# A transformer layer on one core: weight units kept in order, low-rank rows moved by DMA, a new instruction order and no filler matmuls

## What is computed

```python
x = x + xattn(layernorm(x), ctx, ctx)     # 16 batches, 128 tokens, 512 features
x = x + ffn(layernorm(x))
# xattn: RMS norm of q (512) and k (128), rotary, 16 heads of 32 over 4 kv heads,
#        causal softmax, @ w_out.T
# ffn:   w = (w_q - 7.5) * repeat(scale, 64)          4-bit integers held as int32
#        h = relu(xn @ w_up.T + b_up + xn @ a_up @ b_up_lora)      2048 hidden units
#        y = h @ w_down.T + b_down + h @ a_down @ b_down_lora      rank 16
```

## Time and profile before

| | before |
|---|---|
| median of 3 runs | 496.49 us (496.36 to 497.72) |
| the profiled execution, its own time | 496.01 us |
| its span, first to last instruction | 494.2 us |
| PE busy in the span | 462.1 us, 94% |
| DVE, ACT, POOL busy | 348.2, 307.1, 281.3 us |
| mean granted TensorE clock | 0.969 |

### The profile page before, as it was taken

The page is one execution under the profiler, slowest core; times in us unless marked ns, Lnnn a source line. Parts: engine busy times, 40 slices in busy tenths (PEclk is TensorE's granted clock), DMA queues, the critical chain, the costliest instruction groups (busy, mean ns, idle before and its releaser), DMA issues.

```text
span 494.2 us, 8572 instructions
## 1 busy us (share of the span) xinstructions
PE 462.1 (94%) x2569; PEld 229.1 (46%) x2569; DVE 348.2 (70%) x1082; ACT 307.1 (62%) x928; POOL 281.3 (57%) x302
## 2 busy tenths in 40 slices
PE   0774899999999999999999999999999999999997
PEld 0752555545454444444444454545444444444443
DVE  2789999998868685868585868585858675633341
ACT  1499999776766666666676767666666756441110
POOL 3534757847685766565657575857575746460101
PEclk9977589999999999999999999999999999999999
DMA  6883589667786969595969696968787868374523
GB/s 149 313 236 63 183 195 257 104 116 149 140 141 122 173 127 166 99 174 98 197 97 196 98 185 109 175 119 172 115 169 118 158 115 135 76 145 82 86 50 98
DMA packets 207853, 70.43 MB, mean 143 GB/s; under 512 B 197808, under 2 KB 200112, under 8 KB 207120
## 3 DMA queue, kind: packets, MB, share of 16 engines
q1 hardware_dynamic: 205472, 69.33, 69.9%
q10 hardware_dynamic: 2256, 0.40, 0.5%
q0 software_dynamic: 80, 0.16, 0.1%
HBM read 17.44 MB, written 4.19 MB: 44 GB/s over the span
## 4 chain that ended last, share of the span: by engine, by line
PE 78%; DVE 3%; issue 0%
PE ff L949 33%; PE ff L933 32%; PE tb L913 7%; PE sb L881 2%; PE tb L899 2%; DVE big L1073 1%; PE ff L777 1%; DVE wd_lo L1081 1%; PE tb L865 0%; PE ff L837 0%; DVE pr L1179 0%; DVE y L1229 0%; DVE q L1188 0%; DVE z L1110 0%; DVE t_sin L1147 0%
## 5 line engine op out<-in xcount | busy, mean ns | idle before, releaser
L933 PE MATMUL ff<-wu_hi,xnT 128*128 128x512 f16 x512 | 152.4, 379 | 0.0
L949 PE MATMUL ff<-wd_hi,x 128*128 128x512 f16 x512 | 152.3, 379 | 0.0
L1179 DVE CUSTOM_DVE_ANT_0 pr<-sb,tabs,score_scale 128x128 f32<-128x128 f32 x256 | 73.8, 345 | 51.9 <-PE sb L881 51.9
L504 POOL TENSOR_TENSOR big<-pr,big 128x512 f16<-128x512 f32 x64 | 80.1, 1260 | 46.6 <-ACT big L704 46.3
L495 POOL TENSOR_TENSOR pr<-pr,rinv 128x512 f32<-128x512 f32 x64 | 72.0, 1126 | 60.4 <-DVE rinv L1089 60.3
L673 ACT ACTIVATE pr<-pr,nmax 128x128 f32<-128x128 f32 x256 | 98.9, 388 | 7.9 <-DVE nmax L1179 7.9
L933 PE MATMUL ff<-wu_lo,xnT 128*128 128x512 f16 x256 | 97.0, 379 | 0.0
L949 PE MATMUL ff<-wd_lo,x 128*128 128x512 f16 x256 | 97.0, 379 | 0.0
L738 ACT ACTIVATE hid<-z 128x512 f16<-128x512 f32 x64 | 40.0, 626 | 80.0 <-DVE z L1110 80.0
L933 PEld LDWEIGHTS ff<-wu_hi,xnT 128*128 128x128 f16 x512 | 48.2, 98 | 58.8 <-issue 5.9
L949 PEld LDWEIGHTS ff<-wd_hi,x 128*128 128x128 f16 x512 | 49.0, 98 | 54.3 <-DMA x<-hid 0.4
(11 more groups left out here) (153 smaller groups left out, 645.3 us busy)
## 6 DMA issues: line engine op xcount, KB each, us to landing
xt<-in_x SPq DMA_DIRECT2D x16, 256.0 KB, 3.1
big<-in_L_ffn_w_up_q SPq DMA_DIRECT2D x4, 1024.0 KB, 5.9
big<-in_L_ffn_w_down_q SPq DMA_DIRECT2D x4, 1024.0 KB, 5.6
out<-y SPq DMA_DIRECT2D x16, 256.0 KB, 3.0
kvt<-in_ctx SPq DMA_DIRECT2D x16, 64.0 KB, 2.6
wd_lo<-in_L_xattn_w_out SPq DMA_DIRECT2D x1, 1024.0 KB, 9.4
pT<-in_L_ffn_b_up SPq DMA_DIRECT2D x1, 1024.0 KB, 8.6
pT<-big SPq DMA_TRANSPOSE x64, 3.3
```

Of the source, the lines that this page charges most:

```text
L504: pool.tensor_tensor(p3[:, m, :, 1, :], pr[:, m], p3[:, m, :, 0, :], ALU.subtract).then_inc(p_low, 1)
L933: last = pe.matmul(bank[:], a[:, m, :], b[:, m, 512 * g:512 * g + 512], start=(m == 0 and i == 0), stop=(m == KC - 1 and i == 2))
L949: last = pe.matmul(ff[down_bank[n]][:], x2T[:, part, k + h % HG, :], b[:, h, :], start=(h == 0 and i == 0), stop=(h == HC - 1 and i == 2))
L1179: last = dve.tensor_tensor_reduce(pr[:, m, g, :], sbk[m % 2][:, P * g:P * g + P], mask, score_scale[:], 3e38, ALU.add, ALU.min, nmax[:, p, ...
```

## The change

The slot numbers are all new, with two fewer dequantisations and two fewer low parts on VectorE (`DVE_TILES` 26 to 24, `LOW_BY_DVE` 27 to 25). Besides:

```diff
-DVE_TILES = (0, 1, 2, 3, 4, 5, 6, 7, 8, 10, 11, 12, 13, 14, 15, 17, 18, 19, 21, 23, 25, 26, 27, 28, 29, 31)
+DVE_TILES = (0, 1, 2, 3, 4, 5, 6, 7, 9, 10, 11, 12, 13, 14, 15, 16, 17, 18, 21, 23, 25, 26, 27, 29)
+TURN_AT = (10, 30, 64, 91, 234, 258, 301, 449, 504, 516, 568, 619, 656, 687, 732, 750, 775, 784, 902, 976, 1017, 1035, 1078,
+           1084, 1111, 1165, 1188, 1341, 1653, 1726, 1791, 1792)
...
# SyncE: fewer loads first, another order, the rows by DMA
-            load_batch(0)
-            for src, dst in ((kw, kw_bc), (qw, qw_bc)):
+            sp.dma_start(s_dn[:], wds.rearrange("(c p) b -> p c b", p=P)).then_inc(scales_in, 16)
+            for src, dst in ((qw, qw_bc), (kw, kw_bc)):
...
-            for i in range(3):
-                sp.dma_start(b_up_in[R * i:R * i + R], wub).then_inc(b_in, 16)
-                sp.dma_start(b_dn_in[R * i:R * i + R], wdb).then_inc(b_in, 16)
-            sp.wait_ge(scales_in, 16 * 5)
+            load_batch(0)
+            sp.wait_ge(lora_a_in, 16 * 3)
+            sp.wait_ge(norm_w_in, 16 * 2)
             load_group(0)
+            sp.dma_start(wo_raw, wo.rearrange("(j p) c -> p j c", p=P)).then_inc(wout_in, 16)
             load_group(1)
             load_batch(1)
...
+                    if LORA_B_ROWS_AT[i] == s:
+                        sp.wait_ge(b_high, 2)
+                        sp.wait_ge(b_low, 2)
+                        for j in range(3):
+                            sp.dma_start(rows[R * j:R * j + R],
+                                         parts[:, j, :]).then_inc(moved, 16)
...
# ScalarE: low-rank splits on the flat form, 128 partitions; bias row contiguous
-                act.activation(dst, src, ACT.Identity, scale=kap[0:R3, kx:kx + 1]).then_inc(b_high, 1)
+                for parts, flat, kx in ((b_up_parts, b_up_flat, 4), (b_dn_parts, b_dn_flat, 5)):
+                    act.activation(parts[:, 0:2, :], flat.unsqueeze(1).broadcast_to([P, 2, flat.shape[1]]),
+                                   ACT.Identity, scale=kap[:, kx:kx + 1]).then_inc(b_high, 1)
...
# TensorE: no fill() anywhere, and in weights(t)
-                    rows = slice(P * j, P * j + P) if t < UP_TILES else slice(j, None, 4)
-                    last = turn(bank[:, P * i:P * i + P], stage[:, g % W_RING, i, rows],
+                    cols = slice(i, None, 4) if t < UP_TILES else slice(P * i, P * i + P)
+                    last = turn(bank[:, cols], stage[:, g % W_RING, i, P * j:P * j + P],
...
# VectorE: two low parts on the flat form, and another order of the scales
-            input_stats(0)
+            find_tops()
+            norm_powers()
+            gather_tops()
             norm_scales()
             input_moments(0)
-            find_tops()
-            spread_tops()
+            take_tops()
             find_scales()
```

More of the change, by code:

```diff
@@ L48 @@
[L48 to L58, removed]
@@ new lines @@
+R_MOMENTS = (0, 49, 395, 1329)
+R_KEYS = (0, 4, 268, 2190)
+R_POW = (2, 5, 1195, 2191)
+R_CENTRE = (3, 91, 546, 1587)
+R_SINES = (2, 84, 500, 1502)
+R_COSINES = (3, 45, 1206, 2313)
+R_ROPE = (4, 105, 687, 1553)
+R_KSPLIT = (4, 208, 900, 1660)
+R_KLOW = (5, 104, 827, 1624)
+R_KTURN = (259, 483, 1126, 1637)
+R_QSPLIT = (9, 256, 841, 1731)
+R_QLOW = (16, 115, 809, 1605)
+R_QTURN = (152, 503, 951, 1630)
+R_SCORES = ((88, 503, 1006, 1821), (99, 517, 1018, 1850), (124, 593, 1055, 1915), (243, 668, 1110, 1936))
@@ new lines @@
+R_PLOW = ((377, 1378, 2415, 2742), (417, 1440, 2498, 2838), (777, 1570, 2500, 2869), (890, 1619, 2505, 2876))
+R_PTURN = ((529, 1175, 1681, 2031), (741, 1232, 1708, 2041), (761, 1395, 1781, 2052), (798, 1397, 1783, 2058))
+R_VSUM = (496, 524, 922, 1902)
+R_VARG = (341, 433, 1200, 1802)
+R_VPOW = (632, 1469, 2457, 2773)
+R_VSPLIT = (670, 1269, 1936, 2193)
+R_VLOW = (971, 1827, 2712, 2951)
+R_PV = (745, 1312, 1980, 2264)
+R_OHIGH = (735, 1548, 2006, 2305)
+R_OLOW = (689, 1406, 1913, 2207)
+R_PROJ = (752, 1533, 1994, 2293)
@@ new lines @@
+LOAD_AT = (3, 282, 526, 863, 944, 1212)
+ROW_LOAD_AT, DOWN_BIAS_LOAD_AT = 7, 1179
+BATCH_LOAD_AT = (2, 777)
+LORA_BHIGH_AT, LORA_BLOW_AT = 5, 3
+LORA_B_ROWS_AT = (83, 737)
+LORA_TURN_AT = (2, 3, 31)
+LORA_COPY_AT = (12, 13, 72)
+WO_ORDER_AT = (6, 7, 10, 64)
+WO_TURN_AT = (188, 218, 252, 323)
+WO_HIGH_AT = (255, 267, 280, 377)
+WO_LOW_AT = (109, 182, 276, 285)
+LORA_A_AT, LORA_ALOW_AT = 8, 20
+BIAS_ROW_AT = (965, 1355, 1447, 1619)
+WO_SQUARES_AT, WO_SUM_AT, WO_ARG_AT, WO_POW_AT = 11, 22, 45, 17
@@ L423, in _ @@
                         load_group(g)
-                if s == WO_LOAD_AT:
-                    sp.dma_start(wo_raw, wo.rearrange("(j p) c -> p j c", p=P)).then_inc(wout_in, 16)
+                for i, (parts, rows, moved) in enumerate(((b_up_parts, b_up3, b_up_rows), (b_dn_parts, b_dn3, b_dn_rows))):
+                    if LORA_B_ROWS_AT[i] == s:
[4 more added lines that the diff above has]
+                                         parts[:, j, :]).then_inc(moved, 16)
                 for n in (2, 3):
@@ L750, in _ @@
                     lora_a_high()
-                for i in range(5):
-                    if LORA_BHIGH_AT[i] == s:
-                        lora_b_high(i)
+                if LORA_BHIGH_AT == s:
+                    lora_b_high()
                 for i in range(3):
@@ L777, in turn @@
                 return pe.matmul(dst, src, ident[0:src.shape[0], 0:src.shape[0]], is_transpose=True, **kw)
-            def fill(bank, count):
-                for _ in range(count):
-                    pe.matmul(bank[:, 0:P], ident16[:], ident16[:], start=True, stop=True)
             def spread_tops():
@@ L885, in products @@
                 if n is not None:
+                    for m in range(NN):
+                        pe.wait_ge(p_turned[m], 16 * n + 16)
+                    pe.wait_ge(v_high, n + 1)
+                    pe.wait_ge(v_low, n + 1)
                     if n == 0:
@@ L889, in products @@
                         pe.wait_ge(o_low, n)
-                    if n < FREE:
-                        fill(tb[1], PV_FILL[n])
-                    for m in range(NN):
-                        pe.wait_ge(p_turned[m], 16 * n + 16)
-                    pe.wait_ge(v_high, n + 1)
-                    pe.wait_ge(v_low, n + 1)
                     for i, (a, b) in enumerate(((0, 0), (1, 0), (0, 1))):
@@ L1050, in lora_a_low, with lora_b_low @@
                                              ALU.mult, ALU.subtract).then_inc(a_low, 1)
-            def lora_b_low(i):
-                rows = slice(2 * R, R3)
-                dst, src, kx = b_pieces[i]
-                dve.wait_ge(b_high, i + 1)
-                dve.scalar_tensor_tensor(dst[rows], src[rows], kap[rows, kx:kx + 1], dst[rows],
-                                         ALU.mult, ALU.subtract).then_inc(b_low, 1)
+            def lora_b_low():
+                dve.wait_ge(b_high, 2)
+                for parts, flat, kx in ((b_up_parts, b_up_flat, 4), (b_dn_parts, b_dn_flat, 5)):
+                    dve.scalar_tensor_tensor(parts[:, 2, :], flat, kap[:, kx:kx + 1], parts[:, 0, :],
+                                             ALU.mult, ALU.subtract).then_inc(b_low, 1)
             def wout_arg():
@@ L1248, in _ @@
                     lora_a_low()
-                for i in range(5):
-                    if LORA_BLOW_AT[i] == s:
-                        lora_b_low(i)
+                if LORA_BLOW_AT == s:
+                    lora_b_low()
                 for t in range(TILES):
```

231 lines of the change are left out of this document (95 added, 136 removed).

## The result

The changed kernel is slower: 498.88 us against 496.57 us (medians of 20 runs each), ratio 1.0039 with a 95% interval of 1.0023 to 1.0055 (the quotient of the two medians is 1.0047; where a change is told in per cent, the ratio is meant). Medians are of all runs of a kernel; the ratios leave out three runs that were slow as a whole, 561.46 us in e1, 616.3 us in e10 and 2402.21 us of the kernel before. Forecast was 493.8 us and a chance of 0.50 for faster. The time lies in the range, the direction is wrong. In the profiled executions the span grew from 494.2 to 496.4 us. Single runs of one kernel lie a few us apart (the changed kernel's from 495.8 to 500.35), so the ratios of repeated runs decide and the profiles say where.

What follows compares the result with a forecast made beforehand. It took a TensorE never idle from `up(1,0)` at 118.81 us on as the bound. -4.0 + 5.0 - 0.1 - 4.0 + 0.4 = -2.7 us on 496.01, plus 0.5 to the median, gave 493.8 us, range 485.5 to 502.

Steps and rivals of the forecast that it cites:

- Part 4: From `R_PV` to `up(0,0)`: 13.9 us instead of 14.0, -0.1 us, with seven down tiles at 0.81 each.
- Part 3: From the first tile to the first `R_PV`: 15 tiles at half clock plus waits, 41.3 us, +5.0.
- Part 2: Start of the first tile, which waits for the low-rank rows: 26.5 us instead of 30.45, -4.0 us.
- Part 1: Finding the scales at the start: done at 16 us, 3.2 us sooner.
- Part 5: From `up(0,0)` to `up(1,0)`: nine shorter tiles instead of twelve, fewer scores and sums, -4.0 us.
- the work moved behind: One score group and one sum move to behind `up(1,0)`: +0.4 us.
- A: Rival: full clock earlier, VectorE sets the pace in the first tiles; -8 to -11 us, 486 us, chance 0.16.
- B: Rival: up tiles' PSUM writes with a four-word step are slow; +8.5 on the sum, 502 us, chance 0.16.
- C: Rival: rows land at 29 us, half-clocked stretch waits 3 us more; +2.5 + 3, 499 us, chance 0.13.
- D: Rival: later batches no longer close up, 0.4 us missing in each of 14; +5.6, 499 us, chance 0.07.
- E: Rival: the parts cancel, time within 1.5 us of before, 496.5 us, chance 0.14.

Runs made afterwards that it cites:

- e1: Changed kernel with 111 fillers ahead of the first low-rank transposes and 36 ahead of the first tile: 499.11 us, ratio 1.0041 to the kernel before.
- e10: Changed kernel with e3's late bias load, e7's fillers and 20, 10, 60 and 10 fillers ahead of tiles 18 to 21: 492.32 us, ratio 0.9894.
- e2: Changed kernel with 12, 4 and 30 fillers ahead of tiles 18, 19 and 20: 497.12 us, ratio 0.9996 to the kernel before.
- e4: Kernel before with all its fillers left out and nothing else changed: 498.16 us, ratio 1.0041 to the kernel before.
- e3: Changed kernel with the 1 MB bias row loaded later, behind the transpose of the second batch's queries: 495.8 us, ratio 0.9991.
- e7: Changed kernel with e3's late bias load and 20, 12 and 12 fillers in TensorE's idle times at 41, 45 and 50 us: 494.42 us, ratio 0.9975.
- e9: Changed kernel with e3's late bias load, e7's middle fillers and e2's fillers ahead of tiles 18 to 20: 490.92 us, ratio 0.9878.

## Why the prediction was wrong

**The step that failed is Part 4, from `R_PV` to `up(0,0)`: 13.9 us forecast, 19.72 measured.** It took the full clock of before over for the seven down tiles (0.81 each) and put no wait in front of them. The first ones did run at full clock (74.27 to 75.08, 0.81). Then the tiles waited 0.96, 0.24 and 1.94 us for low parts on VectorE: 3.1 us. The clock fell, and the last four took 1.44 us each (83.77 to 85.21) for 0.81, and the three score groups between them 0.57 for 0.32: 3.3 us. The projection gave 1.0 back (2.96 us for 4), and `R_PV` with tile 15 0.2; the remaining 0.6 of the 5.8 is spread over small steps. I had asked of every stretch whether dense work lies ahead that lifts the clock, not whether a wait inside it lets the clock fall again, and I had priced waits in Part 3 alone. e2 shows the clock's part (2.54 us from tile 16 on, 2.1 by the ratios); e4 shows that in the old order the absence of fillers alone does not bring it.

**Part 2, the first tile, was mis-sized: -4.0 forecast, -1.12 measured.** The scales of Part 1 were late, done at 18.58 us and not at 16 (17.43 and 17.50 in e1 and e2, whose code is the same up to there), but the first tile did not hang on them: it starts at 29.3 to 29.7 us whether the rows are issued at 20.1 or at 19.0. It hangs on the queue, as forecast, and the term at fault is the rows' own landing, which I had put at nothing behind the 5.9 MB ahead of them. At 349 GB/s from 9.5 us on, 6.1 MB had moved by 27 us, the forecast's time for the landing; from 27 to 29 us only 117 GB/s moved with the DMA engines busy, and the tile started at 29.33. In e3, with 4.9 MB ahead, they were through at 24.0 us (341 GB/s from 9.5) and the tile started at 26.87, again some 3 us later. Whether the rows' small pieces or the transpose of q, issued at 23.39 us beside them, make these last microseconds slow was not tried.

**Part 3 had the mechanism right, and its matmul work too large.** +5.0 forecast, +1.82 measured. The half clock was there (0.50 in 44 to 70 us), and the waits came to nearly their price: 1.6 us for the third turn of `w_out` (1.3 forecast), 0.9 for tile 5's low part (1.8), and where none was named 0.5 for tile 4's low part and 0.7 for a sum (0.3 for the rest), 3.6 in all for 3.4. TensorE's own work was 34.6 us instead of 37.9. Some 3 us from 40.5 us on ran at full clock, with 1.59 us of matmuls that would have taken twice that; and eight tiles took 1.44 us, not 1.58, since I had priced them by a tile that another tile follows (1.58 us, as from 53.98 to 55.56 here too). These are 1.6 and 1.1 of the 3.3.

**Part 5 was about right**, -4.56 for -4.0, and the work moved behind, +0.36 for +0.4. The sum missed by 4.9: +2.9 in Part 2, -3.2 in Part 3, +5.8 in Part 4, -0.6 in Part 5. That the time lies in the range all the same is in part luck, since the misses of Parts 2 and 3 nearly cancel.

**Rivals.** A (the clock full earlier) did not happen by itself. e7 brought it about and shows what it is worth: `R_PV` 4.3 us sooner than in e3 and the time 0.8, not 8 to 11: from 38 to 61 us TensorE then waits 7 us, nearly all of it for VectorE and ScalarE. B (the strided write slow) is refuted: four transposes with the four-word step take 1.11 us at half clock and 0.66 at full, as the contiguous ones did, and a tile repeats after 1.58 and 0.81. By the Trainium skill, page SBUF — State Buffer, section Door 1: The DMA port swizzle, patterns in PSUM that are not contiguous slow matmuls because of its 8-byte lines; this trace does not agree for such writes. C (first tiles later, or more waits) was nearest in time at 499 us, in part by luck, and half right in its cause: the rows landed at 29 us, its bound; the waits came behind the projection, not in the half-clocked stretch. D (gaps in later batches) is refuted: 100.00 of 100.00 us in 200 to 300. E (the parts cancel, within 1.5 us of before) is not clearly refuted: the ratio gives 1.9 us, with an interval of 1.1 to 2.7.

Left open: why the clock rose by itself at 40.5 us in the profiled execution, and in e2's at 36.6 and again at 63.8 us before any filler. Such differences go with the time: the changed kernel's five runs with a mean granted clock of 0.965 or more took 495.8 to 497.05 us, the fifteen with 0.964 or less 498.08 to 500.35. Its profiled execution is of the second kind, e2's (0.979, where eight of its twelve runs have 0.971 to 0.976) is of its own faster kind, so the two traces lie further apart (4.0 us) than the ratios (2.1).

## What to carry to other kernels

When a change takes fillers out, price each wait twice: once for its idle time and once for the half-clocked work behind it, up to the next dense stretch. Ask this of the new order, not of the old one, since the old order may have stayed up without any filler. A cover pays only as far as the next uncovered wait: the middle fillers were worth 0.8 us alone, within the noise, and 3.9 us when the next wait was covered too. A transfer inside the chip that the first work waits for should not queue behind a megabyte that is first read more than 45 us later (the bias row at 75.8 us, the first tile at 29.33). And price such a transfer's own landing, not only the bytes ahead of it.

## What was not expected of the hardware

- TensorE busy for 16.28 of 18 us (44 to 62 us of the changed kernel) stayed at a granted 0.50, while in e7 it was busy for 13.44 of the same 18 us at 1.00: tiles turned nearly without a gap did not lift the clock, and with 44 fillers in three groups it stayed up in that execution. In e9's and e10's, with the same fillers, it was 0.78 and 0.82 there.
- One idle time did not decide the fall: the clock fell behind 0.96 and 0.24 us in the changed kernel and behind 1.90 in e3, and stayed up behind 1.41 us in e4 and, right after 30 fillers, behind 1.11 in e9.
- In the changed kernel the record reads 1.00 for 31 to 34 us, but the tiles there take 0.60 and 1.11 us, as they do at 0.50. Until its first change the record can't be read; the duration of a known matmul can.
- A write to PSUM with a step of four words cost a transpose nothing (0.66 us for four at full clock, as the contiguous ones); reading the weight block with a step did cost before's down tiles some: four transposes took 0.75 us in e4 against 0.66 now.
